# Rows of 24 tiles per layer fetched by SyncE, one transfer a row, beside GpSimd's indirect gathers

## The reference, cut to what matters

```
h = relu(layernorm(x));  x = x + relu(segment_sum(weight[e] * h[src[e]], dst) @ W2 + b2)    # layer 2
h = relu(layernorm(x));  x = x + segment_sum(h[src[e]], dst) @ W3.T + b3                     # layer 3
```

## Time and profile before

| | us |
|---|---|
| median of 3 runs | 10148.94 (10128.87 to 10150.55) |
| the profiled execution, its own time | 10134.15 |
| span from its first to its last instruction | 10132.3 |
| layer 2, first to last gather issued | 5369.8 to 7717.0 |
| layer 3, first to last gather issued | 7770.6 to 10095.3 |
| POOL busy over the span | 6644.7 (66%) |
| DVE busy | 5034.4 (50%) |
| PE busy | 5196.0 (51%) |

### The profile page before, as it was taken

How to read it: one execution, slowest core, us unless ns; L and a number is a source line. 1 busy time by engine, 2 the same in 40 slices (tenths; PEclk the granted TensorE clock), 3 DMA queues, 4 the chain that set the end, 5 groups by cost and what they waited for, 6 DMA issues and landing times.

```text
span 10132.3 us, 102152 instructions
## 1 busy us (share of the span) xinstructions
PE 5196.0 (51%) x23751; PEld 4130.5 (41%) x23752; DVE 5034.4 (50%) x8799; ACT 2224.9 (22%) x5809; POOL 6644.7 (66%) x6541
## 2 busy tenths in 40 slices
PE   4555555554466666666664444444445444444444
PEld 3333333333366666666663333333333333333333
DVE  5555555554477777777774333333333333333333
ACT  0000000000477777777770000000000000000000
POOL 5666666665488777787785666666665666666665
PEclk7666667676655555555556666667666666666666
DMA  3111111111577777777770000000000000000001
GB/s 67 22 22 22 22 22 22 22 22 32 176 220 220 218 216 219 217 219 218 220 217 19 11 11 11 11 11 11 11 11 16 11 11 11 11 11 11 11 11 16
DMA packets 598627, 724.90 MB, mean 72 GB/s; under 512 B 339211, under 2 KB 432395, under 8 KB 595461
## 3 DMA queue, kind: packets, MB, share of 16 engines
q0 software_dynamic: 289664, 543.79, 21.2%
q1 hardware_dynamic: 308937, 180.80, 6.5%
HBM read 684.32 MB, written 40.12 MB: 71 GB/s over the span
## 4 chain that ended last, share of the span: by engine, by line
another core or an unknown queue 35%; issue 22%; POOL 22%; DVE 14%; DMA 3%; ACT 2%; PE 1%; DVEq 1%; POOLq 0%; SPq 0%; ACTq 0%
POOL arena L502 14%; POOL lanes L502 8%; DVE arena L978 5%; DVE arena L950 3%; DMA lanes<-table,idx 2%; DVE arena L942 1%; DVE lanes L942 1%; DVE lastrow L973 1%; DVE ps L937 1%; DMA arena<-table,idx 1%; ACT arena L699 1%; DVE lanes L968 0%; DVEq L937 0%; DVE ps L1125 0%
## 5 line engine op out<-in xcount | busy, mean ns | idle before, releaser
L502 POOL DMA_INDIRECT lanes<-table,idx x4728 | 4462.5, 944 | 2688.4 <-issue 1409.6
L1214 PE MATMUL ps<-arena,lanes 128*128 128x256 f32 x9456 | 3247.1, 503 | 3710.5 <-DVE arena L950 1710.3
L1214 PEld LDWEIGHTS ps<-arena,lanes 128*128 128x128 f32 x9456 | 2139.5, 247 | 4566.2 <-issue 4208.1
L502 POOL DMA_INDIRECT arena<-table,idx x1664 | 2063.7, 1240 | 657.8 <-issue 604.0
L937 DVE TENSOR_TENSOR ps<-ps,tabs 128x32 f32<-128x32 f32 x1182 | 227.9, 193 | 3326.4 <-remote 3082.4
L551 ACT COPY idx<-tabs 128x4 int32 (+1 forms) x1604 | 301.0, 194 | 6829.8 <-DMA lanes<-table,idx 6483.0
L950 DVE TENSOR_TENSOR arena<-lanes,ps 128x1024 f32<-128x1024 f32 x788 | 959.1, 1217 | 633.0 <-DMA lanes<-table,idx 605.1
L1214 PE MATMUL ps<-lanes 128*128 128x32 f32 x3328 | 791.8, 402 | 702.7 <-issue 500.3
L1214 PEld LDWEIGHTS ps<-lanes 128*128 128x128 f32 x3328 | 750.6, 331 | 729.9 <-issue 729.9
L1311 PE MATMUL ps<-t,arena 128*128 x3328 | 954.3, 401 | 0.0
L1311 PEld LDWEIGHTS ps<-t,arena 128*128 128x128 f32 x3328 | 858.8, 318 | 0.0
(11 more groups left out here) (201 smaller groups left out, 3165.3 us busy)
## 6 DMA issues: line engine op xcount, KB each, us to landing
arena<-step_rows SPq DMA_DIRECT2D x416, 256.0 KB
lanes<-table,idx POOLq DMA_INDIRECT x4728
arena<-table,idx POOLq DMA_INDIRECT x1664
table<-arena SPq DMA_DIRECT2D x24, 1088.0 KB, 4.9
lanes<-in_edge_attr SPq DMA_DIRECT2D x388, 64.0 KB
table<-h SPq DMA_DIRECT2D x18, 256.0 KB, 2.4
edge_rows<-arena SPq DMA_DIRECT2D x1, 2496.0 KB, 8.4
lanes<-self_loop_table,selfi POOLq DMA_INDIRECT x98
```

The lines of the kernel that those rows point to most:

```text
L502: pool.indirect_dma_start(out=to[:, k, u, :], out_offset=None, in_=tableD[l], in_offset=bass.IndirectOffsetOnAxis(ap=idx[:, k, u:u + 1], a ...
L1214: last = mm(ps[:, bass.ds(w[u], rhs.shape[-1])], onehot[:, k, u, :], rhs, start=False, stop=True, skip_group_check=True)
```

## The change: SP fetches 24 tiles of each of layers 2 and 3

The first 24 tiles of layer 2 and of layer 3 are left out of POOL's gathers (`SKIP`, `FIRST`). For each, SP loads 128 row numbers into one partition, reads them in groups of 16 into registers, and starts one transfer of 128 bytes for each edge, into one of two buffers of 128 rows. After every fourth round DVE does the masks, the one-hot matrix and the spreading for one such tile, and PE adds it into the sums. What remains is 97 full rounds (1552 tiles) in place of 98 and a half. DVE's loop body now holds 8 rounds and 2 side tiles, PE's 4 rounds and 1, SP's 2 tiles (256 row transfers). The row numbers are written to DRAM once, at the start. Layers 0 and 1 keep their work.

```diff
+SIDE, PER_SIDE = 24, 4
+SKIP = (0, 0, SIDE, SIDE)
+FIRST = tuple(0 if l == 1 else EXN + SKIP[l] for l in range(4))
...
+LAST_LOTS = tuple(-(-((TILES + EXW - SKIP[l] - 1) % BODY + 1) // HB) for l in range(4))
+C = tuple(STEPS_N // BODY if l == 1 else -(-(TILES + EXW - SKIP[l]) // BODY) for l in range(4))
...
+            sp.dma_start(sideD, sidei[0:SIDE + 1, :]).then_inc(steps_out, 16)
...
+            def side_rows(l):
+                def load(a, j):
+                    sp.dma_start(sideidx[0:1, a, :], sideD[j]).then_inc(side_loaded, 16)
+                sp.wait_ge(table_out[l], BANKS * 16)
+                load(0, slice(0, 1))
+                with sp.Fori(0, SIDE // 2) as i:
+                    for a in range(2):
+                        sp.wait_ge(side_loaded, i * 32 + (16 * (a + 1) + (l - 2) * (SIDE + 1) * 16))
+                        if a == 0:
+                            load(1, bass.ds(i * 2 + 1, 1))
+                        else:
+                            load(0, bass.ds(i * 2 + 2, 1))
+                        for c in range(0, P, 16):
+                            _, rows_of = nc.values_load_multi_w_load_instructions(
+                                sideidx[0:1, a, c:c + 16], engines=(mybir.EngineType.SP,), min_val=0,
...
+                            if c == 0:
+                                sp.wait_ge(side_msg, i * 2 + (a + 1 + (l - 2) * SIDE))
+                            for u, r in enumerate(rows_of):
+                                sp.dma_start(siderow[c + u:c + u + 1, a, :], tableD[l][bass.ds(r, 1), :]
+                                             ).then_inc(side_gathered[l - 2][a], 16)
...
             put_table(2)
             put_windows(windowW)
+            side_rows(2)
             put_table(3)
+            side_rows(3)
...
+            def side_tile(l, i, a):
+                n = i * 2 + (a + (l - 2) * SIDE)
...
+                dve.wait_ge(side_done, n + 1)
+                tt(sidemask, iota_ps[:, 0:WB], col(tabs[:, BLK, :]).to_broadcast([P, WB]), ALU.is_equal
+                   ).then_inc(side_masked, 1)
+                tt(sidehot, iota_ps, col(node).to_broadcast([P, P]), ALU.is_equal)
...
+                if l == 2:
+                    tt(sidewmask, sidemask, col(tabs[:, WGT, :]).to_broadcast([P, WB]), ALU.mult
+                       ).then_inc(side_masked, 1)
...
+                dve.wait_ge(side_gathered[l - 2][a], i * (16 * P) + 16 * P)
+                tt(sidemsg, siderow[:, a, :].unsqueeze(1).to_broadcast([P, WB, D]),
+                   (sidewmask if l == 2 else sidemask).unsqueeze(2).to_broadcast([P, WB, D]), ALU.mult
+                   ).then_inc(side_msg, 1)
...
+                    with dve.Fori(0, SIDE // 2) as i:
+                        for a in range(2):
+                            for j in range(PER_SIDE):
+                                body(i * (2 * PER_SIDE) + (a * PER_SIDE + j), LOTS)
+                            side_tile(l, i, a)
...
+            def side_scatter(l, i):
+                w = windows(i, 1, each=1)
+                pe.wait_ge(side_msg, i + (3 + (l - 2) * SIDE))
+                mm(ps[:, bass.ds(w[0], WB * D)], sidehot, sidemsg.rearrange("p w f -> p (w f)"), start=False, stop=True,
+                   skip_group_check=True).then_inc(side_done, 1)
...
+                    with pe.Fori(0, SIDE) as i:
+                        for j in range(PER_SIDE):
+                            body(i * PER_SIDE + j)
+                        side_scatter(l, i)
```

More of the change, by code:

```diff
@@ L215, in gnn @@
                        for a in range(2))
+        sidemask, sidewmask = (ps[:, W7 + 2 * BODY * WB + a * WB:W7 + 2 * BODY * WB + (a + 1) * WB] for a in range(2))
         iota_ps = ps[:, W7 + BANK - P:W7 + BANK]
@@ L303, in gnn @@
         coef_ready = pairwise("coef_ready")
+        side_loaded = sem("side_sources_loaded")
+        side_gathered = [[sem(f"side_rows_gathered{l}_{a}") for a in range(2)] for l in (2, 3)]
+        side_masked = sem("side_masks_ready")
+        side_msg = sem("side_msg_ready")
+        side_done = sem("side_scatter_done")
         stored = sem("output_stored")
@@ L509, in _ @@
                 if l != 1:
-                    body(BEFORE[l + 1], LAST_LOTS)
+                    body(BEFORE[l + 1], LAST_LOTS[l])
         @block.scalar
@@ L600, in next_lot @@
             def next_lot(l, i, k, end):
-                if end and l != 1 and k >= LAST_LOTS:
+                if end and l != 1 and k >= LAST_LOTS[l]:
                     act.wait_ge(idx_ready[k], BEFORE[l + 1])
@@ L1122, in body2 @@
                     masks(2, i, k)
-                    onehots(i, k, onehot)
+                    onehots(i, k, onehot, 2)
                     dve.wait_ge(masked[k], i + (C[0] + 1))
-                    tt(wmask[:, k], mask[:, k], per_edge(WGT, i, k), ALU.mult).then_inc(weighted[k], 1)
+                    tt(wmask[:, k], mask[:, k], per_edge(WGT, i, k, 2), ALU.mult).then_inc(weighted[k], 1)
                     dve.wait_ge(gathered[2][k], i * 64 + 64)
@@ L1200, in clear, with windows @@
                        skip_group_check=True)
-            def windows(i, n):
+            def windows(i, n, first=0, each=BODY):
                 _, w = nc.values_load_multi_w_load_instructions(
-                    window[0:1, bass.ds(i * BODY, n)], engines=(mybir.EngineType.PE,), min_val=0,
+                    window[0:1, bass.ds(i * each + first, n)], engines=(mybir.EngineType.PE,), min_val=0,
                     max_val=(BLOCKS - 1) * D, skip_runtime_bounds_check_because="windows of nodes below N_NODES")
@@ L1220, in scatter, with body @@
                 last.then_inc(mm_done[k], 1)
+            def side_scatter(l, i):
[3 more added lines that the diff above has]
+                   skip_group_check=True).then_inc(side_done, 1)
             def scatters(l):
-                with pe.Fori(0, C[l] - 1) as i:
-                    w = windows(i, BODY)
+                def body(i):
+                    w = windows(i, BODY, SKIP[l])
                     for k in range(LOTS):
                         scatter(l, i, k, w[k * HB:], wmsg)
-                w = windows(C[l] - 1, LAST_LOTS * HB)
-                for k in range(LAST_LOTS):
+                if l == 0:
+                    with pe.Fori(0, C[l] - 1) as i:
+                        body(i)
+                else:
+                    with pe.Fori(0, SIDE) as i:
+                        for j in range(PER_SIDE):
+                            body(i * PER_SIDE + j)
+                        side_scatter(l, i)
+                w = windows(C[l] - 1, LAST_LOTS[l] * HB, SKIP[l])
+                for k in range(LAST_LOTS[l]):
                     scatter(l, C[l] - 1, k, w[k * HB:], wmsg)
```

43 lines of the change are left out of this document (29 added, 14 removed).

## The result

| | before | after |
|---|---|---|
| median, us | 10138.91 (10121.64 to 10150.55) | 11882.48 (11878.96 to 11894.25, 4 runs) |
| ratio to before, 95% interval | | 1.1719 [1.17, 1.1738] |
| the profiled execution, its own time | 10134.15 | 11894.25 |
| span | 10132.3 | 11892.4 |
| layer 2, first to last gather | 5369.8 to 7717.0 | 5361.3 to 8558.4 |

The changed kernel is 17% slower. It is rival 1 of the prediction, to which 0.12 had been given. The span grew by 1760.1 us: layer 2 by 849.9, layer 3 by 860.6; the stretch between them, 53.6 before, is 79.1, and behind the last gather are 69.6 us where there were 37.0, because DVE waits for the rows of each layer's last side tile (42.5 us in layer 2, until 8593.9) when POOL has already ended; and layer 2 began 8.5 us earlier. Layers 0 and 1 are as before.

What follows compares the result with a forecast made beforehand. The bound was taken as POOL's gathers at 1.248 us plus a 7.4 us stop in about every 32. The terms, -71.2 + 6 + 1 = -64 us, took the 10148.9 median to 10085 us; range 10040 to 10210.

Steps and rivals of the forecast that it cites:

- rival 1: SP becomes the bound, seen at DVE's wait for `side_gathered`: from 0.66 us a row; at 0.8, 10970 us; chance 0.12.
- SP's work, against its time: SP's row fetching in layers 2 and 3: 65 us a tile at 0.42 a row, hidden under 79.9 or 94.9 us.
- rival 2: POOL's stops grow if SP's transfers delay PE's `mm_done`: 10239 us at a fifth more, 10470 at half; chance 0.12.
- Gathers removed: POOL in layers 2 and 3: 24 gathers less in each, -71.2 us; -59.9 if stops stayed as many.
- DVE's side tile: DVE's masks, one-hot and spreading for a side tile: 1.3 us each, mostly hidden, one in ten charged, +6 us.
- PE's: PE's register load and product for a side tile: about 2 us in 95, cost none, up to 96 us.
- start: Row numbers written by SP under cover of a wait, one small copy more on DVE: +1 us.
- DMA load: 128 small packets a side tile on the DMA engines beside POOL's gathers: cost none.
- The long loop on SP: SP's loop exceeds the 512 instructions held, so every two-tile turn would begin with a fetch stall; not priced.
- Rivals 3 and 4: Side tiles' DVE and PE time all on the path, 10140 us, chance 0.1; POOL's stops shrink, 9931 us, chance 0.08.

Runs made afterwards that it cites:

- experiment 5: Changed kernel with POOL gathering only the first of the four tiles of each lot in layers 2 and 3: 8612.4 us against 10059.02, ratio 0.8554.
- experiment 1: Changed kernel with one transfer of 128 neighbouring rows a side tile in place of 8 register loads and 128 transfers: 10011.8 us against 10059.02, ratio 0.9944.

## Why the prediction was wrong

*SP's work, against its time* is the step that failed: "I take 0.42 us" a row, 65 us a tile, "hidden, with 30 us to spare". The size was right for an engine left alone (0.41 us a row, 61 us a tile without the hold, and the same with it once POOL gathers less, in experiment 5). What failed is the condition: it was laid beside POOL's 80 us of gathers as if the two were independent. On this chip SP starts 10 rows in the slow 35 us of a run of 28 gathers, so a tile waits for POOL's stops, and the stops must be made long enough for it.

Rival 1 was named with the right place and the right deciding point (DVE's wait for `side_gathered`, 0.66 us a row). Its price, 883 us, was worked out from 0.8 us a row, as a slower constant rate; measured are 3.5 us beside POOL's runs and 0.41 without, and DVE waits 44.3 us a tile, 2125.4 us in all. POOL's idle time on DVE rose by less, 2550.6 - 770.1 = 1780.5 us in both layers, since some of the stops of before fall into these waits. Two rows on record spoke for it and were given too little weight. In layer 1, SP's MOVE has a median of 0.029 us and a longest of 0.700, and a register move moves no data for which it could be late. It starts at 2714.49, among gathers 1.25 us apart, and in the kernel before on a chip without the hold the longest is 0.029:

```profile
L417 SPq MOVE arena<-step_rows x416: 29/29/29, 2194.3 to 4787.9; - x139
```

(The longest transfer, 1.187 us in the earlier trace rows, says nothing: there it is 1.332.) And DVE waited 12.74 us for PE's signal with nobody to name as releaser. The prediction said of that, "nobody in the trace explains this", put it down as rival 2, in which SP would harm the signal, and did not ask the reverse: whether what delays PE's signal would delay SP. The medians were read, the longest were not followed to their time, though where that 0.7 us move lies against POOL's gathers was to be had from the trace of before.

*Gathers removed* (-71.2, near end -59.9), *DVE's side tile* (+6), *PE's* (0) and *start* (+1): right together, -64 forecast, -56 [-74, -37] measured by experiment 1 with the stops present, and 8883.04 - 8820.43 = 62.6 without them, where only 59.9 were on offer by the pitch. 1552 gathers a layer, as said. Without the hold the side tile on DVE is never seen on the path: in the second kind of chip its spreading has no idle time before it and POOL none behind it.

*DMA load* (no cost): right. Gathers take 0.944 us beside SP's transfers on the second kind of chip, where the change gains what its gathers are worth. Constant rows, the same packets, cost 0.65% with the hold, which holds up their instructions too: DVE waits 375.3 us for them.

*The long loop on SP*: of the Trainium skill's rule (Runtime: NRT & Kernel Launch, section Instruction fetch mechanics), that a taken branch out of what the engine holds waits for a fetch, this much is seen: the instruction queue q14 moved 1.79 MB in 219 packets, before 0.11 MB in 14. It costs nothing that shows here: the same 1.79 MB flow where the change gains 62.6 us.

```profile
q14 instruction: 219, 1.79, 0.1%
```

*Rival 2* (stops grow): the wait for PE's signal is 1064.7 us in layer 3 against 1161.1, so it didn't grow. *Rivals 3 and 4* fall with experiment 1. The range to 10210 took in rival 1 only up to a rate just over 0.66 us; with a signal nobody could explain in the very stretch, it should have been priced from the longest rows, not the median. (The range's "10148.9 - 74" should be 70, 71.2 less the 1 us of the start; that changes nothing.)

What stays open: what the hold is. The runs show where it is (SP's or ACT's instructions when they issue rows, and PE's signals; mostly from 3 to 4 us into a run of gathers at 1.25 us to 4 to 5 us after it), that with less work on PE it shows on POOL and DVE instead, what lifts it (gathers further apart, or gaps), and that some chips don't have it. That late signals and slow instructions have one cause is argued from their coming and going together, on the same chips and at the same times (8099.30 and 8099.47), and not shown by itself. The runs don't show which shared thing is taken.

## What to carry to other kernels

An idle engine isn't free capacity: ask how fast its instructions go at that time, and read the longest durations of cheap instructions (moves, fulfilled waits) against the busy engine's timeline before the median. Where a wait has no releaser that the profile can name, whatever delays it may delay the new work too. When a gain hangs on such a thing, measure on more than one chip: the same change was 17% slower on one and 0.7% faster on another.

## What was not expected of the hardware

- The kernel before takes 10059 to 10151 us on some chips and 8883 on others. The second kind shows the same gather (0.944 us, pitch 1.248) and the same DVE, with no late signals; the stops of the earlier trace rows come with the hold, and the kernel alone doesn't make them.
- In a run of gathers, from 3.5 us after its start (8059.83 to 8063.36) to 4.8 us after its end (8094.54 to 8099.30), 31 instructions of SP stood 1.16 us apart, register operations and moves as well as transfers, while ACT's register operations took 0.046 to 0.069 us.
- With a quarter of PE's products POOL's stops go, but its gathers take up to 1.636 us instead of 0.957.
- A one-row transfer with its row in a register costs SP 0.225 + 0.037 + 0.029, 0.41 us with gaps; with registers for source and target 0.529 us for the transfer alone.
- 16 fulfilled waits of POOL between two gathers cost nothing on a chip without the hold (1.0001 [0.9991, 1.0011]), 28 cost 17%.
- A register load of 16 values takes SP 1.228 us in the median (0.077 a register), near PE's 0.069.
